# Second MLP product cut into three parts across the turn's end, and the last exponential of a turn before the logarithm

## What is computed

```python
def _ln(x, s, b):                       # over the 96 channels of a token
    m, v = mean(x), var(x)
    return (x - m) * rsqrt(v + EPS) * s + b

def _vit(t):                            # t: windows x 49 tokens x 96
    h = _ln(t, ln1_s, ln1_b)
    q, k, v = h @ wq + bq, h @ wk + bk, h @ wv + bv        # 12 heads of 8
    attn = softmax(q k^T / sqrt(8))
    t = t + (attn v) @ wo + bo
    h = _ln(t, ln2_s, ln2_b)
    return t + gelu(h @ w1 + b1) @ w2 + b2                 # 96 -> 384 -> 96

x = x + depthwise_conv_31x31(_gn(x), weight) + bias_term
x = x + windows_back(_vit(windows(roll(_gn(x), -3))))      # 7 x 7 windows
```

## Time and profile before

| | us |
|---|---|
| three runs | 5706.78, 5679.43, 5709.63 (median 5706.78) |
| the profiled execution | 5688.4 |
| its span, first to last instruction | 5686.6 |
| mean granted TensorE clock in it | 0.976 of full |
| PE busy | 5342.2 (94%) |
| ACT, POOL, DVE busy | 3542.0, 3509.3, 3397.2 |

### The profile page before, as it was taken

The page is one execution under the profiler, slowest core; times in us unless marked ns, Lnnn a source line. Parts: engine busy times, 40 slices in busy tenths (PEclk is TensorE's granted clock), DMA queues, the critical chain, the costliest instruction groups (busy, mean ns, idle before and its releaser), DMA issues.

```text
span 5686.6 us, 229687 instructions
## 1 busy us (share of the span) xinstructions
PE 5342.2 (94%) x97360; PEld 4217.5 (74%) x97360; DVE 3397.2 (60%) x5850; ACT 3542.0 (62%) x5590; POOL 3509.3 (62%) x4814
## 2 busy tenths in 40 slices
PE   6999999999599999999999999999999999999998
PEld 6999999999466666666666666666666666666665
DVE  2333333433267677677676777776677777777773
ACT  3444444444367777777776777777777777777775
POOL 2222222222367777777777777777777777777774
PEclk9999999999689999999998999999999999999996
DMA  4444444444356666666665666666666666666662
GB/s 125 116 121 120 127 121 120 116 125 104 71 126 140 140 140 140 140 140 140 140 140 127 139 139 140 140 140 140 140 140 140 140 140 140 140 140 140 140 140 47
DMA packets 1099823, 740.58 MB, mean 130 GB/s; under 512 B 465428, under 2 KB 1070708, under 8 KB 1098708
## 3 DMA queue, kind: packets, MB, share of 16 engines
q1 hardware_dynamic: 1069620, 687.18, 53.6%
q0 software_dynamic: 29184, 38.71, 3.2%
HBM read 409.02 MB, written 316.46 MB: 128 GB/s over the span
## 4 chain that ended last, share of the span: by engine, by line
PE 61%; issue 7%; DVE 3%; ACT 3%; POOL 0%; ACTq 0%; DVEq 0%; POOLq 0%
PE ps_pv L1121 14%; PE ps_ring L1188 8%; PE ps_s L1075 5%; PE ps_ring L1058 4%; PE ps_xc L1163 4%; PE ps_ring L1049 4%; PE ps_t L1075 4%; PE ps_ring L1180 4%; PE ps_ring L1066 4%; PE ps_ring L1060 2%; PE ps_ring L1059 2%; DVE b_rest L983 2%; ACT b_sq_hi L848 2%; PE ps_ring L1149 2%; PE ps_ring L1067 2%
## 5 line engine op out<-in xcount | busy, mean ns | idle before, releaser
L940 DVE TENSOR_REDUCE b_mx<-ps_s 113x12 f32<-113x588 f32 x1024 | 783.9, 766 | 200.6 <-PE ps_s L1075 200.4
L1121 PEld LDWEIGHTS ps_pv<-b_vd,b_probs_t 128*64 128x64 f32 x24576 | 771.1, 140 | 164.0 <-issue 155.1
L840 ACT ACTIVATE b_probs_t<-ps_t 128x588 f32<-128x588 f32 x1024 | 667.7, 652 | 303.0 <-PE ps_t L1075 302.9
L225 POOL TENSOR_SCALAR xn<-xin,aff 96x896 f32<-96x896 f32 x192 | 173.4, 903 | 1072.2 <-DVE aff L375 1059.5
L1121 PE MATMUL ps_pv<-b_vd,b_probs_t 128*64 128x18 f32 x24576 | 822.5, 213 | 0.3 <-issue 0.3
L746 POOL TENSOR_TENSOR b_mid_lo<-b_mid,b_mid_hi 128x392 fp32r<-128x392 f32 x768 | 788.9, 1027 | 43.3
L410 PE MATMUL ps_conv<-blocks_hi,toep_hi 128*128 128x288 f32 (+2 forms) x2880 | 667.2, 313 | 0.0
L410 PE MATMUL ps_conv<-blocks_hi,toep_lo 128*128 128x288 f32 (+2 forms) x2880 | 654.4, 309 | 0.0
L410 PE MATMUL ps_conv<-blocks_lo,toep_hi 128*128 128x288 f32 (+2 forms) x2880 | 653.7, 308 | 0.0
L801 POOL TENSOR_TENSOR b_outs<-b_y,b_xs 96x392 f32<-96x392 f32 x256 | 316.7, 1237 | 445.2 <-DVE b_y L1021 445.2
L282 ACT ACTIVATE toep_hi<-toep 128x640 fp32r<-128x640 f32 x288 | 197.2, 749 | 632.9 <-PE ps_conv L410 616.7
(11 more groups left out here) (142 smaller groups left out, 12423.3 us busy)
## 6 DMA issues: line engine op xcount, KB each, us to landing
stacked_qk<-b_planes SPq DMA_DIRECT2D x512, 220.5 KB, 2.9
b_q_st<-stacked_qk SPq DMA_DIRECT2D x512, 220.5 KB, 4.3
b_k_st<-stacked_qk SPq DMA_DIRECT2D x512, 220.5 KB, 5.6
toep<-filters_padded SPq DMA_DIRECT2D x96, 936.5 KB, 14.0
stacked_qk<-b_planes SPq DMA_DIRECT2D x512, 147.0 KB, 2.4
stacked_qk<-b_planes SPq DMA_DIRECT2D x512, 73.5 KB, 1.9
b_xs<-x_scratch SPq DMA_DIRECT2D x224, 147.0 KB, 2.8
out<-b_outs SPq DMA_DIRECT2D x224, 147.0 KB, 3.2
```

Of the source, the lines that this page charges most:

```text
L840: act.activation(pt[:, p, 0:HEADS * TOK].rearrange("k (e n) -> k e n", e=2), ps_t[:, :, 0:HPAIR * TOK], ACT.Exp, scale=float(DH) ** -0.5). ...
L940: dve.tensor_reduce(mx[0:rows_q, :].rearrange("q (e m p) -> q e m p", e=2, p=PAIRS)[:, :, :, p], ps_s[0:rows_q, :, 0:HPAIR * TOK].rearrang ...
L1121: ins = pe.matmul(to, pt[:, p, at:at + WS], vd[:, m % VR, p, h, :, :], start=True, stop=True, skip_group_check=True)
```

## The change

The nine products of the second MLP leave the end of the turn and become three calls of `contract` in the next turn: one ahead of `below_max` 0, one between it and the centring, one after the centring. `held` is the strip that was at MLPS one turn ago. ACT takes the exponential of `below_max` 3 ahead of the logarithm of var2. The orders of DVE, POOL and SP are the same instruction for instruction, so `y` keeps its place in DVE's turn. (The changed file holds the text of `window_pass` twice; the second definition replaces the first, and the difference between it and the one before is this.)

```diff
@@ scalar, step @@
                 if qkv is not None:
                     act.wait_ge(S["k_ps"], qkv + 1)
                     act.activation(planes[:, 0, 1, :], bank(i, s, "k")[0:C, 0:NT], ACT.Copy).then_inc(S["k_high"], 1)
+                exps(i, soft, 3)
                 if proj is not None:
                     log_var(proj, bank(i, s, "var2"), "var2", "lg2")
                 if proj is not None:
                     act.wait_ge(S["h1_done"], qkv + 1 if qkv is not None else BATCH * B)
                     inv_std(proj, "lg2", "rstd2")
-                exps(i, soft, 3)
@@ tensor @@
+            def contract(i, s, n, m):
+                if n is None:
+                    return
+                if m == 0:
+                    wait_bank(pe, i, s, "w2")
+                pe.wait_ge(S["mid_split"], NM * n + m + 1)
+                for k, (w, src) in enumerate(((w2_hi, mid_hi), (w2_lo, mid_hi), (w2_hi, mid_lo))):
+                    ins = pe.matmul(bank(i, s, "w2")[0:C, 0:NT], w[:, m, :], src[:, m, :],
+                                    start=(m == 0 and k == 0), stop=(m == NM - 1 and k == 2))
+                if m == NM - 1:
+                    ins.then_inc(S["w2_ps"], 1)
+
             def step(i, s):
                 qkv, att, soft, proj, mlps = (strip(i, s, x) for x in (QKV, ATT, SOFT, PROJ, MLPS))
+                held = strip(i, s, MLPS + 1)
+                contract(i, s - 1, held, 0)
                 below_max(i, soft, 0)
+                contract(i, s - 1, held, 1)
                 if qkv is not None:
...
                     pe.matmul(ps_xc[0:C, 0:NT], centre[:, :], t0_lo[:, qkv % 2, :], start=False,
                               stop=True).then_inc(S["xc1"], 1)
+                contract(i, s - 1, held, 2)
                 scores(i, att, 0)
...
                     ins.then_inc(S["v_ps"], 1)
-                if mlps is not None:
-                    wait_bank(pe, i, s, "w2")
-                    for m in range(NM):
-                        pe.wait_ge(S["mid_split"], NM * mlps + m + 1)
-                        for n, (w, src) in enumerate(((w2_hi, mid_hi), (w2_lo, mid_hi), (w2_hi, mid_lo))):
-                            ins = pe.matmul(bank(i, s, "w2")[0:C, 0:NT], w[:, m, :], src[:, m, :],
-                                            start=(m == 0 and n == 0), stop=(m == NM - 1 and n == 2))
-                    ins.then_inc(S["w2_ps"], 1)
```

More of the change, by code:

```diff
@@ new lines, in _, with convolve, step @@
+        @block.tensor
+        def _(pe):
+            pe.wait_ge(const_loaded, 32)
+            def convolve(par, dy):
+                y0, y1 = max(0, -dy), min(NYB, NYB - dy)
+                for dx in (0, -1, 1, -2, 2):
+                    for data, taps in ((blocks_hi, toep_hi), (blocks_lo, toep_hi), (blocks_hi, toep_lo)):
+                        for e in range(2):
+                            outs = [b for b in range(e, NXB, 2) if 0 <= b + dx < NXB]
+                            first, n = outs[0], len(outs)
+                            to = ps_conv[:, 2 * par + e, :].rearrange("p (j n) -> p j n", n=P)
+                            ins = pe.matmul(
+                                to[:, first // 2:first // 2 + n, y0 * BATCH:y1 * BATCH],
+                                taps[:, par, 1 + dy, NDX // 2 + dx, :],
+                                data[:, par, first + dx:first + dx + 2 * n - 1:2, (y0 + dy) * BATCH:(y1 + dy) * BATCH],
+                                start=(dy == 0 and dx == 0 and data is blocks_hi and taps is toep_hi),
+                                stop=(dy == 1 and dx == 2 and taps is toep_lo), skip_group_check=True)
+                return ins
+            def step(i, s):
+                g = B * i + s
+                for ch in range(GC):
+                    k = GC * (s - 1) + ch
+                    c = GC * (g - 1) + ch
+                    if ok(i, k + 1, GC * B):
+                        ch1, gs = (ch + 1) % GC, s - 1 if ch < GC - 1 else s
+                        if ch1 == 0:
+                            pe.wait_ge(normed, B * i + gs + 1)
+                        if not (isinstance(i, int) and c + 1 < 1):
+                            pe.wait_ge(tin_done, c + 1)
+                        for b in range(NXB):
+                            ins = pe.transpose(ps_tr[:, b // 4, (b % 4) * P:(b % 4 + 1) * P], xn[:, gs % 2, ch1, b, :],
+                                               cc("ident"))
+                        ins.then_inc(tin_ps, 1)
+                    if ok(i, k, GC * B):
+                        pe.wait_ge(t_split, c + 1)
+                        pe.wait_ge(tin_done, c + 1)
+                        if not (isinstance(i, int) and c < 2):
+                            pe.wait_ge(conv_copied, c - 1)
+                        convolve(k % 2, 0)
+                    if ok(i, k - 1, GC * B) and not (isinstance(i, int) and c < 2):
+                        pe.wait_ge(x1_done, c - 1)
+                    if ch == 0 and ok(i, s, B):
+                        pe.wait_ge(sums_done, g + 1)
+                        if not (isinstance(i, int) and g < 1):
+                            pe.wait_ge(var_done, g)
+                        pe.matmul(moments_at(s), cc("samebatch"), sums[:, s % 2, :],
+                                  start=True, stop=True).then_inc(moments, 1)
+                    if ok(i, k - 1, GC * B):
+                        pe.wait_ge(conv_copied, c)
+                        for b in range(NXB):
+                            ins = pe.transpose(ps_tr[:, 2 + b // 4, (b % 4) * P:(b % 4 + 1) * P],
+                                               conv_sb[:, slot_of(b):slot_of(b) + P], cc("ident"))
+                        ins.then_inc(turned, 1)
+                    if ok(i, k, GC * B):
+                        convolve(k % 2, -1)
+                        convolve(k % 2, 1).then_inc(conv_ps, 1)
+            steps(pe, step)
+            pe.wait_ge(fin_v, 1)
+            for q in range(2):
+                ins = pe.matmul(ps_tr[0:C, 0, q * BATCH:(q + 1) * BATCH], sums1c[:, q, :], cc("batchsum"), start=True,
+                                stop=True)
+            ins.then_inc(fin_p, 1)
```

510 lines of the change are left out of this document (added).

## The result

| us | before | changed |
|---|---|---|
| median of 20 runs each | 5700.87 | 5722.92 |
| lowest and highest of them | 5679.43 to 5727.08 | 5713.44 to 5732.06 |
| profiled execution, span | 5688.4, 5686.6 | 5729.51, 5727.7 |
| mean granted clock in it | 0.976 | 0.977 |

The ratio is 1.0036, with a 95% interval from 1.0026 to 1.0047: slower by 0.4%, under the 0.5% that was to count as a change. The forecast was 5725.

The account below looks back on a forecast made before the run. A ring over POOL, `sq2_lo`, var2 and `y` was taken to set the turn, with PE close to the bound but not it. 5688.4 + 57 (`y` later) - 13 (clock) - 7 (draining) = 5725 us, range 5682 to 5754.

Parts of the forecast that it names:

- The ring: `y` releases POOL's work to the last `mid_lo`, which holds `sq2_lo`, then var2, `h2`, `y`: claimed to set the turn.
- the image turn: Turn where a new image begins: one 0.18 us POOL copy more lengthens it by 0.24, taken to show POOL sets the turn.
- `y` 0.23 later a turn: Third part behind the centring, which waits for `h2`: `y` at 3014.64 instead of 3014.41, 249 x 0.23 = 57 us.
- ACT: The exponential, about 0.65, goes into 1.22 us ahead of the logarithm: cost nothing; without that cover 0.65.
- `below_max` 1: On PE after scores 0: a 0.17 wait for the exponential goes, and it starts 0.02 later than now.
- The clock: Two half-clock falls in the steady part, 5.3 and 7.9 lost, both go: -13.2, bounds 0 to -13.2.
- five products where two stood: Five products of 392 columns between `below_max` 0 and scores 0 shorten the sparse run, so both clock falls go.
- no half clock between 1700 and 5500: Sign that the forecast is right: no half-clock stretch in that span of the changed kernel's profile.
- The rival that the clock falls more often: PE's idle before var2 grows from 0.66 to about 0.9; 6.6 per fall, over 5738 from two falls; chance 0.20.
- the changed kernel's runs agree more closely: If the half-clock falls go, the changed kernel's runs should agree closely; runs before span 30.
- Draining: Last turns: `below_max` 1's exponential wait goes, -2.4, and clock worth -5; together -7, between 0 and -14.

Follow-up runs that it names:

- The dose: Kernel before, with POOL's 0.18 us group norm copy made in every turn instead of once an image: 5749.85, ratio 1.0085.
- the cut: Kernel before, with one wait added on POOL so its last `mid_lo` follows `sq2_lo`: 5622.78, ratio 0.9874.
- PE's edit alone: Changed kernel with ACT's last exponential put back behind `rstd2`: 5880.93, ratio 1.0336 against the kernel before.
- ACT's edit alone: Kernel before, with only ACT's last exponential moved ahead of the logarithm of var2: 5705.47, ratio 0.9999.
- the better order on PE: Changed kernel with the third part of the products ahead of the centring instead of behind it: 5669.86, ratio 0.995 against the kernel before.

## Why the prediction was right

**The ring (right).** The dose, the cut and the table show what the image turn only suggested. The hold of `mid_lo` on `sq2_lo` is as the rule of the Trainium skill has it ("SBUF — State Buffer", section "SBUF: two separate sides"). In the trace DVE's instruction is on record as begun and busy, and in 246 of 256 strips of the kernel before it ends 0.42 or 0.43 after POOL's, whatever its own start. The trace also bears out that the operands decide. `sq2_lo` reads two from SBUF. The scaling of the attention's result (`b_o`, L954), also a DVE instruction on two tensors, reads one of them from PSUM; in 229 of 231 steady turns it begins while POOL is at a subtraction of 1.02 us (L754), and it is never held (durations in ns as above):

```profile
L954 DVE TENSOR_TENSOR b_o<-ps_pv,b_rden x256: 556/558/559, 1582.5 to 5660.0; 128x384 f32<-128x384 f32 x128
```

So it is not just any work on POOL that slows DVE. That the ports are the reason, and not another tie that goes by the same operands, rests on that page; no run here separates them.

**`y` 0.23 later a turn (right in its mechanism, too large).** It is 0.18 (turns of 15.98 and 16.22 for the 16.03 and 16.27 forecast): 44.7 over the steady part, 45 over all 249 turns, instead of 57. The whole error is the first step: from the end of `h2` to the centring I put the 0.15 that lies between the subtraction from q and var2. The trace has 0.10 there, while var2 still follows its subtraction by 0.15 (3209.79 to 3209.94). Why the two differ is open. The steps behind it, 0.23 (for 0.22), 0.18 and 0.04, came as predicted.

**ACT (right).** The exponential fills 1.22 us of idle time and delays nothing. I did not price what its absence would do to `below_max` 0, which the text only named. That is 0.37 a turn.

**`below_max` 1 (right).** It starts 0.18 behind scores 0 (3213.97 to 3214.15) and waits for nothing.

**The clock (wrong against the profiled execution).** Both long stretches at half clock went, as I had it. The reason that I gave, five products where two stood, is not shown: PE's edit alone has the same five, and in its profile three stretches of 13.7 to 20.5 us begin behind the narrow products. And "no half clock between 1700 and 5500" did not hold: eight short ones came behind the longer idle time before var2, worth 12.4 together, so that -13.2 became -1.1. The rival that the clock falls more often named this place, but priced a fall at 6.6; a short one costs 12.4 / 8 = 1.6. Against the medians of the runs the term looks better: they differ by 22, not 41, since the profiled execution of the kernel before is one of its faster ones. That this is the clock is likely: in 17 more runs of that kernel the mean granted clock goes from 0.977 in the fastest (5683.06) to 0.966 in the slowest (5735.38), and the kernel with ACT's edit alone, whose turn is the same, had five falls worth 30 in its profile. That the changed kernel's runs agree more closely came true: 20 of them lie within 18.6, those of before within 47.7.

**Draining.** -3.8 for -7, within its bounds. The wait of `below_max` 1 for the exponential is gone from these turns (2.8 in four of them before, put at 2.4), which leaves about 1 for the clock, put at 5.

The forecast lies 2 us from the median, and that is partly luck: the ring's term was 12 too high and the clock's 12 too low, against the profiled execution. It also started from an execution 12 below the median of its kernel: from there it forecast 37 more, and from median to median the change is 22.

## What to carry to other kernels

An engine that is busy 60% of the time can still set the turn, if its chain closes a ring: look for the instruction whose duration varies while its shape does not, and for what ends a fixed time ahead of it. Where DVE and POOL meet like that, let the one that others wait for go first: one wait on POOL was worth 1.3% here, and 2.3% in the changed kernel (5722.92 to 5591.16), more than the better order on PE gained (0.9% without that wait, 5722.92 to 5669.86, and 0.6% with it, 5591.16 to 5557.26). And a producer that is moved past a wait takes that wait along: count from the end of the wait to the consumer, and compare with when the consumer was free.

## What the runs showed that was not expected

- The half clock comes in two kinds here: stretches of 13.7 to 20.5 us behind the narrow products, with PE never idle in the records (13.70 busy of 13.70 in the earlier trace rows), and stretches of 3.4 us, 1 to 3 us behind the 0.8 to 1.1 us of idle time before var2, mostly where that was over 1.0. Two stretches in the profile of PE's edit alone fit neither: 30.7 and 54.6 us, begun 1.4 and 2.4 us behind that idle time. The kernels that idle 0.33 there had none of the short kind but one; the kernels with the new order on PE that also have ACT's edit had none of the long kind in the steady part.
- With the ring cut, the profile of the kernel before has five of the long kind (39 us of longer turns) though PE idled less, as many as that with ACT's edit alone, where PE idled 0.66. What brings such a stretch about stays open.
- The same kind of step, from DVE's end to a matmul that waited for it, took 0.15 at var2 and 0.10 at the centring in one turn.
- POOL's final sum may be held too, by `h2_lo`, which on DVE reads two operands from SBUF and begins 0.16 ahead of it. In all nine kernels it takes 1.2 us or more but for the very last, behind which no `h2_lo` runs: 0.97. The kernel before, in ns as above:

```profile
L801 POOL TENSOR_TENSOR b_outs<-b_y,b_xs x256: 966/1238/1254, 1621.7 to 5682.7; 96x392 f32<-96x392 f32 x128
```

That would be 0.27 of POOL's time in each turn. No run moves `h2_lo`, so this is not shown.
